# Key and value taps split before the preceding sums, and four of nine blank fills issued in the token attention's section

## The reference, cut to what matters

```
q, k, v = conv3x3(x, Wq), conv3x3(x, Wk), conv3x3(x, Wv)
att  = softmax over m of (einsum('nchw,mchw->nmhw', q, k) / sqrt(C))
virt = einsum('nmhw,mchw->nchw', att, v)
virt = relu(normalise each image of virt, scale gamma, shift beta)
x    = x + conv3x3(virt, Wc)

t = tokens of x (16 x 256 of 128 numbers)
t = t + compositional_attention(layer_norm(t), ...)   # 8 searches, 2 retrievals
t = t + experts(layer_norm(t), Wg, W1, W2)            # 8 experts, top 2 of each token
```

## Time and profile before

| What | Value |
|---|---|
| Median of three runs | 733.07 us (732.03 to 736.17) |
| The profiled execution's own time | 733.24 us |
| Its span in the trace | 731.3 us |
| PE busy | 604.4 us (83% of the span) |
| DVE busy | 475.4 us (65%) |
| ACT busy | 307.7 us (42%) |
| POOL busy | 264.2 us (36%) |
| Transfers | 105.48 MB, mean 144 GB/s |

### The profile page before, as it was taken

How to read it: one execution, slowest core, us unless ns; L and a number is a source line. 1 busy time by engine, 2 the same in 40 slices (tenths; PEclk the granted TensorE clock), 3 DMA queues, 4 the chain that set the end, 5 groups by cost and what they waited for, 6 DMA issues and landing times. The chain is left out here.

```text
span 731.3 us, 11228 instructions
## 1 busy us (share of the span) xinstructions
PE 604.4 (83%) x3562; PEld 521.7 (71%) x3562; DVE 475.4 (65%) x1240; ACT 307.7 (42%) x619; POOL 264.2 (36%) x296
## 2 busy tenths in 40 slices
PE   5699999838788999989799897987519999999930
PEld 4488888626588998879689787976407888888820
DVE  5675784755557678767758575775535777767725
ACT  3221222223345353534425253433108778878710
POOL 3041454567000101131413213145550567666670
PEclk9899999959879999999989998997558999999965
DMA  8999444530431404050311305000029677777209
GB/s 258 374 362 356 163 157 141 177 130 0 144 116 30 145 1 145 2 174 1 120 55 60 115 1 173 2 30 31 30 75 344 226 238 238 249 252 226 74 8 344
DMA packets 55224, 105.48 MB, mean 144 GB/s; under 512 B 8744, under 2 KB 21689, under 8 KB 55040
## 3 DMA queue, kind: packets, MB, share of 16 engines
q1 hardware_dynamic: 50176, 96.24, 39.8%
q0 software_dynamic: 4992, 8.54, 3.3%
HBM read 58.15 MB, written 48.42 MB: 146 GB/s over the span
## 5 line engine op out<-in xcount | busy, mean ns | idle before, releaser
L1568 PE MATMUL bank<-rvx,s_expd 128*128 128x96 f32 x1024 | 140.6, 285 | 13.3 <-ACT s_expd L1020 9.4
L1568 PEld LDWEIGHTS bank<-rvx,s_expd 128*128 128x128 f32 x1024 | 134.1, 204 | 16.5 <-ACT s_expd L1020 11.4
L1020 ACT ACTIVATE s_expd<-bank 128x512 f32<-128x512 f32 x128 | 75.7, 598 | 125.2 <-PE bank L1552 102.0
L1215 DVE TENSOR_REDUCE s_max<-bank 128x2 f32<-128x512 f32 x128 | 87.1, 689 | 57.5 <-PE bank L1531 44.3
L1872 POOL DMA_INDIRECT y_slots<-virt,pad_l x92 | 96.4, 1048 | 71.7 <-DVE virt L1923 39.3
L905 POOL TENSOR_TENSOR ln_rstd<-ln_var,power 128x4 f32<-128x4 f32 x17 | 17.4, 1025 | 201.5 <-DVE ln_var L1191 201.5
L936 POOL DMA_INDIRECT x_slots<-rows,slot_of x64 | 62.9, 983 | 64.6 <-DVE rows L1343 40.8
L1911 DVE TENSOR_TENSOR k_stack<-virt,k_stack 128x512 fp32r<-128x512 f32 x92 | 63.4, 689 | 28.4 <-ACT k_stack L1891 24.2
L53 PE MATMUL bank<-pad_h,u_h 128*128 128x512 f32 x144 | 60.9, 423 | 14.5 <-DVE pad_l L395 8.2
L1552 PE MATMUL bank<-q_stack,k_stack 100*128 100x256 f32 x256 | 62.4, 328 | 5.2 <-DVE q_stack L1233 5.2
L1886 ACT ACTIVATE virt<-bank 128x512 f32<-128x512 f32 x92 | 54.5, 592 | 17.9 <-PE bank L55 16.5
(11 more groups left out here) (251 smaller groups left out, 1227.8 us busy)
## 6 DMA issues: line engine op xcount, KB each, us to landing
x_slots<-blank SPq DMA_DIRECT2D x8, 2112.0 KB, 20.9
pad_h<-w_split SPq DMA_DIRECT2D x23, 512.0 KB
q_stack<-w_split SPq DMA_DIRECT2D x23, 512.0 KB
qk_rows<-qk SPq DMA_DIRECT2D x16, 512.0 KB
k_stack<-qk_rows SPq DMA_DIRECT2D x96, 64.0 KB, 2.1
q_stack<-qk_rows SPq DMA_DIRECT2D x48, 128.0 KB, 2.4
pad_l<-x_slots SPq DMA_DIRECT2D x23, 264.0 KB
e_raw<-in_w SPq DMA_DIRECT2D x16, 256.0 KB, 2.9
```

Source lines behind the costliest of these rows:

```text
L1020: nc.scalar.activation(expd[:, s % 2].rearrange("p a i -> p (a i)"), ps_st[s % 2][:, :], ACT.Exp).then_inc(exp_done, 1)
L1215: nc.vector.tensor_reduce(s_max[:, :, s], ps_s[s % 2][:, :].rearrange("p (a j) -> p a j", a=2), AX.X, ALU.max).then_inc(max_done, 1)
L1568: last = pe.matmul(ps_pv[s // 4][:, at:at + RVW], expd[:, s % 2, a, i * P:(i + 1) * P], rvx[:, ring, 2 * b + a, :], start=(a == 0), stop=( ...
```

## The change: what it does

Two things change. First, the lists of DVE and ACT in round 0 are written in another order: the taps of keys are made ahead of the sums of queries, and those of values ahead of the sums of keys. Second, SP issues five of the nine blank fills where it issued nine, and the other four as the first entries of its list in the third section. The wait at the end of the first section counts five. POOL waits for all nine ahead of its first scatter. The tile `blank` and the semaphore `blanked` are now made by the outermost function, so that they live through all sections.

```diff
+BLANKED_EARLY = 5
+
+def blank_expert(eng, x_slots, blank, e):
+    first, n = (e * CAP, CAP // CH) if e < NE else (NE * CAP, SPARE)
+    dst = x_slots[first:first + n * CH].rearrange("(k p j) f -> p k (j f)", p=P, j=G)
+    rows = blank[:, :, :].rearrange("p j f -> p (j f)").unsqueeze(1).broadcast_to([P, n, G * ROW])
+    return eng.dma_start(dst, rows)
...
             sp.wait_ge(blank_steps, 2)
-            blank_rows = blank[:, :, :].rearrange("p j f -> p (j f)")
-            for first, n in [(e * CAP, CAP // CH) for e in range(NE)] + [(NE * CAP, SPARE)]:
-                dst = x_slots[first:first + n * CH].rearrange("(k p j) f -> p k (j f)", p=P, j=G)
-                sp.dma_start(dst, blank_rows.unsqueeze(1).broadcast_to([P, n, G * ROW])).then_inc(blanked, 16)
+            for e in range(BLANKED_EARLY):
+                blank_expert(sp, x_slots, blank, e).then_inc(blanked, 16)
...
-            sp.wait_ge(blanked, 16 * (NE + 1))
+            sp.wait_ge(blanked, 16 * BLANKED_EARLY)
...
@@ ACT, round 0 @@
             mix_high(0, 3)
-            keep_one(0, 0)
             for n in (1, 2):
                 outer_high(n)
                 middle_high(n)
-                keep_one(0, n)
-                if n == 1:
-                    mix_high(1, 0)
-                    mix_high(1, 1)
+                keep_one(0, n - 1)
+            mix_high(1, 0)
+            mix_high(1, 1)
+            keep_one(0, 2)
             mix_high(1, 2)
...
@@ DVE, round 0 @@
             mix_low(0, 3)
-            mixed_halves(0, 0)
-            even_rows(0, 0)
             middle(1)
-            odd_rows(0, 0)
             outer_low(1)
             middle_low(1)
+            gather(0, 0)
             middle(2)
-            gather(0, 1)
             outer_low(2)
             middle_low(2)
+            gather(0, 1)
             for t in range(4):
                 mix_low(1, t)
...
@@ token attention, SP @@
+        for e in range(BLANKED_EARLY, NE + 1):
+            blank_expert(sp, x_slots, blank, e).then_inc(blanked, 16)
         sp.wait_ge(stack_init, 2)
         stack(0, 0)
...
@@ token attention, POOL @@
         def scatter(u, ring, halves=(0, 1)):
+            if u == 0:
+                pool.wait_ge(blanked, 16 * (NE + 1))
```

More of the change, by code:

```diff
@@ L58, in conv_attention @@
 def conv_attention(nc, sb, sem, bank, pad_h, pad_l, resid, virt, ident, wc_h, wc_l, x_chwn, x_cnhw, w_qkv, w_c, stats, ones,
-                   power, ret_blocks, late_loads, d_wkretT, consts, f_w1, f_w2, w_split, x_slots, resid_loaded):
+                   power, ret_blocks, late_loads, d_wkretT, consts, f_w1, f_w2, w_split, x_slots, resid_loaded, blank,
+                   blanked):
     NS = NCH // 2
@@ L82, in conv_attention @@
         e_high = sb("e_high", [P, 2, CH], F32R, ctx)
-        blank = sb("blank", [P, G, ROW], where=ctx)
         count8 = sb("count8", [P, 4, NE], I32, ctx)
@@ L135, in conv_attention @@
         blank_steps = sem("blank_steps")
-        blanked = sem("blanked")
         const_steps = sem("const_steps")
@@ L682, in token_attention @@
                     wvr, wqr_t, ret_blocks, wout, wg, qk_rows, consts, tile_list, out, x_slots, scattered,
-                    listed, resid_loaded):
+                    listed, resid_loaded, blank, blanked):
     S, D = 8, 16
@@ L2047, in mixed_kernel @@
         resid_loaded = sem("resid_loaded")
+        blank = sb("blank", [P, G, ROW])
+        blanked = sem("blanked")
         scattered = [sem("scattered0"), sem("scattered1")]
@@ L2055, in mixed_kernel @@
                            w_qkv, w_c, stats, ones, power, ret_blocks, late_loads, wkretT, consts, f_w1, f_w2, w_split,
-                           x_slots, resid_loaded)
+                           x_slots, resid_loaded, blank, blanked)
             image_norm(nc, sb, sem, bank, pad_h, pad_l, stats, gb, ones, power, norm_a, norm_b)
@@ L2061, in mixed_kernel @@
                 nc, late, block, sb, sem, bank, pad_h, pad_l, resid, virt, ident, wc_h, wc_l, norm_a, norm_b, power, wq,
-                wk, wvr, wqr_t, ret_blocks, wout, wg, qk_rows, consts, tile_list, out, x_slots, scattered, listed, resid_loaded)
+                wk, wvr, wqr_t, ret_blocks, wout, wg, qk_rows, consts, tile_list, out, x_slots, scattered, listed,
+                resid_loaded, blank, blanked)
             experts(nc, block, sem, bank, pad_h, pad_l, q_stack, k_stack, virt, resid, ident, tile_list, listed,
```

## The result

The changed kernel took 725.3 us (median of four runs, 724.31 to 726.4), the kernel before 732.8 us on the same chip: ratio 0.9894, 95% interval 0.9866 to 0.9923. So it is faster by 7.5 us, where 9.9 were forecast. The profiled execution's span fell from 731.3 to 724.5 us.

The account below looks back on a forecast made before the run. PE, the busiest engine, was taken to wait for keys' and values' taps in the first section; 9.9 + 0 + 0 = 9.9 us off 733.24 gives 723.3 us, own range 721.5 to 725.5, overall 720.8 to 728.5.

Parts of the forecast that it names:

- Holes and their low clock, 9.9 us: First section: PE's two waits for keys' and values' taps close, and the low clock behind them goes, gaining 9.9 us.
- the keys' hole: First section: PE's 3.91 us gap between matmuls, waiting for the keys' taps, closes with 1.0 us to spare.
- DVE starts `middle(1)` at 13.82 and ends it 1.62 later: First section: DVE's moved additions for keys end at 15.45, so the keys' last rest ends at 17.3.
- that meeting of the two engines: First section, from 28.3 us: POOL working beside DVE slows a pair of `mix_low` by 0.9 us; cost taken as 0.
- The tightest place, near 41 us: Round 1: PE's first `turn`, about 41.1, needs DVE's softmax and last values' sum; costs 0 to 1 us, taken as 0.
- Why part two matters: End of first section: without moving four fills, stores land at 148.6 and 8.6 of the 9.9 us are lost.
- part one: First section, round 0: the new order of taps gains 9.9 us, or 6.7 us without the clock's share.
- PE shows no hole there: Around 90 us: DVE and ACT waited for POOL's late `mix(3)` but PE did not; moving fills alone worth about 0.
- the fourth rival: Entering the third section beside fills costs 1 us for fetching code: 724.3 us, chance inside the forecast's 0.74.
- Stores of weights: First section: with four fewer early fills, the last store of expert weights is issued near 130, landing about 133.6.
- Fills in the third section: Third section: four fills start at 149.4, end by 173.8 to 175, before the first stack store at 176.0; cost 0.
- Everything behind shifts: Behind the first chunk everything stays the same and moves earlier with the 9.9 us gain.

Follow-up runs that it names:

- e3: The changed kernel run again without edit, on another chip: 698.3 us, ratio 0.9864 against the kernel before.
- e10: The changed kernel with seven fills early and two late: 698.82 us, ratio 0.9876 against the kernel before.
- e7: The changed kernel with POOL's rows of round 1 held back until DVE made the rests of the keys' taps: 697.9 us, ratio 0.9882 against the kernel before.
- e9: The changed kernel with all nine fills early and POOL's rows of round 3 made ahead of expert-weight piece 2: 706.83 us, ratio 1.0012 against the kernel before.
- e1: The changed kernel with the new order of taps but all nine fills in the first section: 706.74 us, ratio 0.9992 against the kernel before.
- e4_before_again: The kernel before run once more without edit, a single execution: 709.05 us.
- e5: The changed kernel with no fill early, all nine in the token attention's section: 722.0 us, ratio 1.0232 against the kernel before.
- e6: The changed kernel with POOL's third memset of the ones' rows put behind DVE's `z_tok`: 694.7 us, ratio 0.9839 against the kernel before.

## Why the prediction was right, and where it failed

The sum was 9.9 us, and the profiled execution gained 6.84 (733.24 to 726.4): 1.6 less at round 1, 0.6 more at the end of the first section, 2.5 less at the start of the third, 0.4 more behind it. The medians differ by 7.5, inside the range.

- *Holes and their low clock, 9.9 us.* Measured at round 1: 8.3 us, and 8.55 between two traces on another chip. The holes were priced rightly; the term that was too large is the closing of the keys' hole, and the failed step is "DVE starts `middle(1)` at 13.82 and ends it 1.62 later". It took the durations from a place where POOL was idle. In the new place POOL's mixes for round 1 run beside it (they wait for DVE's `mix_low`, and so start within 0.3 us of DVE's additions), and the two slowed additions took 2.1 us more. Of that PE lost what its own slow start left over: its keys began 0.15 us late behind queries in the first trace, 0.7 in e3, 1.2 in e10 (18.18 and 19.65), and not late in e7. The other part of the 1.6 us is the slow start of the first trace (1.3 us), which no term of the sum allowed for. The prediction weighed that meeting of the two engines, but only from 28.3 us on. Undone in e7: round 1 at 37.11.
- *The tightest place, near 41 us.* Right: PE shows no wait there. Beside POOL, DVE's `probs` took 1.36 us, within its slack.
- *Why part two matters.* The size was right (part one alone gains nothing, part two alone nothing), the reason was half of it. That the stores of weights would hold the section is shown by e9. But "PE shows no hole there" was read as slack, where it was a bound met exactly: the rows of round 3 were due at the moment they came, and with PE 8.4 us earlier they cost 6 us of standing still and a low clock (e1). ACT's wait of 7.47 us for them in the trace of before was the sign.
- *The end of the first section.* The stores were closer than the prediction read. It put the last store's landing at 148.6 by the median of 3.5 us, but this one took 5.2 and landed at 150.3, behind DVE's end at 149.9. So in that trace the store ended the section, and most of the 0.89 us that the fourth rival took for the price of entering was the wait for it: in `e4_before_again` it landed 0.5 us ahead of DVE's end, and the wait was 0.31. These are the 0.6 us more.
- *Stores of weights.* Forecast issue near 130, measured 130.37.
- *Fills in the third section.* Right: the last was issued at 155.34 and took 19.0 us, so it landed at 174.3 (173.8 to 175 forecast), 5.2 us ahead of the first store. PE's wait for the stacks was 2.60 us against 2.27. With five fills more they cost 23 us of waiting (e5).
- *Entering the third section beside fills.* No cost in any run. From DVE's start in the second section to ACT's in the third it was 8.55 us, and 8.54 before.
- *Everything behind shifts.* Not so in the profiled execution, which lost 2.5 us at the start of the third section: 0.4 until `z_tok` was ready, and 2.1 from there to the first store, at a low clock that two other executions of the same program don't have. The gain in the medians on the other chips was 8.6 and 10.8 us, around the 8.9 us that e3 and e4 differ by at the first store of stacks. That the total came so near the forecast rests in part on luck: the spread between executions is as large as the terms that were missed.
- *The range.* The words for its low end (1 us below 721.5) give 720.5, and 720.8 is stated; nothing hangs on it.

## What to carry to other kernels

Before an operation is moved, look at what the other engines do at its new time, and price it by a row with the same neighbour; here DVE's additions took 0.55 us beside an idle POOL and 1.6 beside its two-operand work. A hole in the busiest engine can have several bounds behind it: follow each producer of the next stage and ask when it would come too late. An engine between it and the busiest one that already waits (here ACT, 7.5 us) is a sign that there may be no slack. A part that gains nothing alone may be what lets another gain.

## What the runs showed of the hardware that was not expected

- A POOL memset of 3.51 us slowed DVE's `z_tok`, four operations with one SBUF tensor operand each, from 1.1 to 4.19 us. Beside the same memset, moved behind `z_tok` in e6, DVE's `t_chunk` (which reads PSUM) and its `zt_l` (which reads two SBUF tensors) kept 0.69 us each. But `tensor_tensor` operations with two SBUF tensors did slow down beside POOL's `tensor_tensor`: the keys' additions, 0.55 to 1.56 and 1.67 us.
- Around the same 2.94 to 2.99 us wait of PE the granted clock fell in five traces (`z_tok`'s transposes 1.11 to 1.12 us in four of them) and stayed at 1.00 in six (0.66 us).
- The chip of the first comparison ran the kernel before 24 to 27 us slower than the three others did, and the changed kernel 27 us slower than two of them. In both traces from it ACT stands still for 3 to 5.6 us several times in the third section, with DVE and PE idle for part of it; the waits name a releaser that the profile doesn't know. Of the changed kernel, ACT's waits (us in total, times, longest):

```profile
ACT s_expd L1026 <- remote: 24.3, 7, 5.5
```

No trace of the other chips has such a wait. Their cause stays open.
